# A four-stage sequence model: attention stacks moved in halves, a second pair of score banks for the last sequence, and its own instruction order for the first and last sequences

## The chip, the cores and the metric

One core of one Trainium2 chip runs the whole program. The metric is the device time of one execution in microseconds; the kernel before has a median of 1859.53 us over three runs (1855.02 to 1859.66). Of the engines, PE is TensorE, DVE VectorE, ACT ScalarE, POOL GpSimd, and SP issues the DMAs.

## What is computed

Sixteen sequences of 512 tokens with 128 channels pass through four residual stages, each behind a layernorm:

- **s**, a selective scan: `h = exp(delta*A)*h + x*x` over time for 256 channels with 16 states each, then the sum over states, gates, and a projection back to 128.
- **g**, eight linear experts with a softmax gate over the residual norms, of which the best two count.
- **t**, causal attention with 16 heads. Query and key of a head have 8 plain and 4 rotated dimensions; `attn = softmax(QK/sqrt(12)) V`, then a projection.
- **f**, a gated feed-forward net with three layers of width 512 and the output projection.

## The kernel before, in words

`one_pass` builds two phases. Phase one holds s, g and t of all sequences, phase two holds f. The engines are programmed by hand: each function such as `pe_scores` (L938) or `dve_scans` (L557) is a generator, a *strand*, that issues the instructions of one stage of one sequence on one engine, with its semaphore waits, in steps set off by `yield`. `in_order` (L197) merges the strands of an engine: step k of a strand of sequence b is due at `PERIOD * b + TIMES[name][k]`, and the step that is due first is issued next. The due times (L51 to L143) set nothing but this order. When a step runs is decided by its waits and by what stands ahead of it in the queue of its engine. Since a sequence's strands reach over some 3.5 periods, in the middle of phase one scans of one sequence, the experts of an earlier and the attention of a still earlier one are interleaved.

The parts around the change:

- *Scans.* Per sequence 32 scans (L566, DVE), whose decays come from ACT (L551) and whose results POOL adds up (L584). They need `dve_s_head` (L495), which needs the first projection `pe_s_head`.
- *Start.* `dve_setup` (L1124) step 0 makes the centering matrix (L1128) from the loaded identity; `pe_setup` (L1154) folds it into the weights of s, ACT copies the result back (L1096), and only then can the first projection run. Steps 3 and 4 (L1138), 5 (L1148) prepare the weights of g.
- *Experts.* `dve_g_gate` step 2 (L744 to L771) ends with the weights of the experts. PE transposes them (L647), ACT copies them (L701), PE adds the biases (L655), ACT copies (L706); then PE issues expert products (L669) into banks 3 and 4 in turn, and DVE accumulates each with four instructions (L790, `dve_g_experts`). Product e waits for the accumulation of product e-2.
- *Attention inputs.* `pe_t_proj` (L807) and `act_t_proj` (L850) make query and key of all heads in `parts`, DVE and POOL (L881, L901) the rotated rows in `rest`. Heads must lie on 12 neighbouring partitions, so `sp_rows` (L349) moves them by DMA into `stacks`, even heads at partition 0, odd heads at 64, eight pairs behind one another: two DMAs of 64 KB for the rotated queries (L360), two for the rotated key, broadcast over the pairs (L362), and four of 128 KB for the plain rows (L368). It first waits for the last score step of the sequence before, which reads the same buffer.
- *Scores.* `pe_scores` takes 4 groups of 4 heads in 5 steps each. A step fills a double bank of PSUM (`self.scores`, banks 5 and 6, 1024 columns); `act_scores` (L955) takes the exponential of it with one instruction (L967) into `probs`. There is one double bank, so each step waits for the exponential of the step before (`a_prob`).
- *Values.* Each group has three units (steps 0 and 1, 2 and 3, and 4). POOL masks the diagonal blocks of a unit (L1011), PE multiplies with the values (L1028). `probs` has two buffers: a unit's exponentials wait for the values of the unit two before. After a group ACT copies the sums (L982), PE transposes them (L1035), DVE divides (L1068, L1070). After the fourth group: PE, ACT and PE again (L1049, L986, L1055) and the addition to x (`dve_t_out`, L1078), then the moments for f (`dve_f_moments`, L380).

Phase two waits for all of phase one (`phase_one_over`). The program also holds a general version of both phases in a branch that the inputs here do not take.

The functions that the diff touches:

Of the kernel before, what the change touches and what calls it, by code (L numbers as in the profile page):

```python
# [6 lines left out]
F32 = mybir.dt.float32  # L7
# [7 lines left out]
P = 128  # L15
# [7 lines left out]
DQK = DH + DR  # L23
# [27 lines left out]
PERIOD, F_PERIOD = 78826, 24000  # L51
TIMES = {
    "sp_loads": [-193999],
    "sp_rows": [236612, 244449, 262646],
    "sp_weights": [202048],
    "pe_setup": [-253368],
    "pe_s_out": [105457],
    "pe_scores": [203061, 206712, 210127, 211906, 212752, 218421, 220191, 221756, 225635, 230028, 233012, 236030,
        238938, 243841, 244836, 246508, 250105, 253149, 258508, 260547],
    "pe_bound": [265919],  # L60
    "dve_setup": [-65717, -48779, -18943, -17968, -16808, -12885],
    "dve_scans": [-5373, -4435, -1891, 334, 3476, 5244, 7204, 9355, 13725, 15210, 17850, 18956, 19850, 22896, 23940,
        25115, 29162, 29883, 31506, 34450, 37022, 37715, 39471, 43460, 46148, 47755, 48770, 50392, 51830, 53721,
        55818, 56579],
    "dve_s_out": [36751, 66351, 104857],
    "dve_f_moments": [285358],
    "dve_bound": [265666],
    "act_setup": [-109930, -101590],
    "act_decays": [-9159, -8011, -5609, -4706, -4216, -2340, -1414, -1286, 2396, 2947, 3280, 4612, 4837, 7344, 10757,
        11123, 26812, 27582, 27750, 29700, 31063, 33980, 34333, 34908, 36535, 38255, 39294, 39719, 40895, 41965,  # L70
        43611, 44575],
    "act_inputs": [-9090, 28279],
    "act_f_rstd": [294212],
    "pool_setup": [-159627],
    "pool_sums": [-5156, -2015, 3236, 4530, 7688, 11440, 13004, 16496, 18832, 24903, 25813, 29142, 29865, 31310,
        34155, 34495, 35661, 37442, 38619, 41328, 41420, 41788, 43639, 46579, 47169, 48256, 51750, 53260, 54332,
        56586, 59092, 62805],
    "pool_t_proj": [181583],
    "pool_masks": [205555, 210959, 214428, 221911, 231307, 234364, 239298, 241162, 247591, 257454, 259145, 261183],
# [5 lines left out]
    "dve_clips": [205554, 210958, 214427, 221910, 231306, 234363, 239297, 241161, 247590, 257453, 259144, 261182],  # L85
    "pe_s_turn": [-44316],
    "pe_s_head": [-29204, -17779, -6800, 16442],
# [3 lines left out]
    "pool_s_head": [-19406, -10949, 18784, 22665],  # L91
    "pe_values": [210177, 216686, 219526, 221752, 223371, 231041, 234330, 237530, 242565, 246311, 247251, 251115,
        258893, 263255, 264524, 267412],
    "pe_t_out": [270351, 271838],
    "dve_values": [222049, 239132, 250423, 268172],
    "dve_t_out": [284589],
    "act_scores": [202759, 207082, 211090, 212302, 214034, 217813, 222387, 223555, 227340, 230817, 234204, 238260,
        240384, 242483, 245583, 249636, 251803, 255073, 257206, 258841],
    "act_nums": [220127, 235782, 250419, 265886, 272466],
# [17 lines left out]
    "pe_g_turn": [111532],  # L117
    "pe_g_residuals": [114116, 119481, 119533, 119540, 122328, 126496, 128548, 129135],
    "pe_g_own": [143450, 146011],
    "pe_g_experts": [149181, 150687, 152499, 155319, 156674, 157680, 161416, 164909],  # L120
    "act_g_rstd": [109296],
    "act_g_turned": [113955],
    "act_g_squares": [115694, 118311, 119742, 121869, 123757, 126271, 129317, 132198],
    "act_g_gate": [134222, 138635, 145715, 147184],
    "act_s_rstd": [-106834],
    "act_s_turned": [-35041],
    "act_s_xn": [-104074],
    "act_g_xn": [109881],
    "act_t_xn": [172512],
    "dve_g_norm": [106445],  # L130
    "dve_g_sums": [117932, 121419, 122771, 126327, 127060, 128048, 131606, 133569],
    "dve_g_gate": [134799, 136597, 141564],
    "dve_g_experts": [152123, 154366, 154898, 157601, 159574, 160538, 161592, 161722, 164119],
    "pe_t_turn": [173660],
    "pe_t_proj": [176180, 179691, 183932, 186365, 186842, 189324],
    "act_t_rstd": [171027],
    "act_t_turned": [174285],
    "act_t_proj": [184944, 186825, 187429],
    "dve_t_norm": [164962],
    "dve_t_proj": [176579, 178912, 188307, 191093],  # L140
    "pe_g_setup": [-14755, -8586, -4947, -2930, 3681, 17023],
    "act_g_setup": [-8024, -702, 28025, 63003, 104601],
    "pe_t_setup": [-3990, 26455, 88672],  # L143
    "act_t_setup": [30456, 43692, 102220],
# [1614 lines left out]
```

## Time and profile before

| | |
|---|---|
| median of three runs | 1859.53 us |
| the profiled execution | 1853.92 us |
| its span, first to last instruction | 1849.2 us |
| around the span | 4.7 us |
| mean granted clock of PE | 0.951 of full speed |
| busy over the span: PE, DVE, ACT, POOL | 82%, 83%, 70%, 60% |
| phase one, until the last addition to x | 0 to about 1454 us |
| first and last scan | at 29.8 and 1260.1 us |

Times in rows are us from the start of the span. A timeline row has start, duration, engine, line and operation, output<-inputs, sizes and a count; neighbours of one kind are merged, and in brackets stands how long the engine sat idle before and what released it.

### The profile page before, as it was taken

The numbers are of one execution on the slowest core, as the hardware profiler recorded it, in microseconds if no ns is written. First come the engines' busy times: TensorE is split into PE (matmuls) and PEld (weight loads), VectorE is DVE, ScalarE is ACT, GpSimd is POOL, SyncE is SP. The second block draws the span as 40 slices with busy tenths as digits, with TensorE's granted clock in tenths as the row PEclk, the third lists the DMA queues.
The fourth block names the chain that finished last, engine by engine and source line by source line (L and its number), as shares of the span: only waits on it lengthen the run. The fifth ranks groups of instructions, "written<-read, shape, count | busy, mean of one in ns | idle before, by whom it ended". The sixth has DMA issues, their size and how long they took to land. (4 is left out here: it accounts for less than half of the span.)

```text
span 1849.2 us, 24467 instructions
## 1 busy us (share of the span) xinstructions
PE 1518.6 (82%) x8039; PEld 807.2 (44%) x8039; DVE 1541.3 (83%) x2837; ACT 1286.7 (70%) x2176; POOL 1112.0 (60%) x987
## 2 busy tenths in 40 slices
PE   4246888888888888888888888888886699999997
PEld 2022333333433333343333334333332478888886
DVE  5899999999999999999999998996330488988883
ACT  5666898888888888888888888884543444444441
POOL 4885775858677585866758686674111255555552
PEclk9566999999999999999999999999998799999998
DMA  4000110101001010100101010010400000000000
GB/s 131 0 1 4 15 17 1 18 1 18 7 12 18 1 18 1 18 8 11 18 1 18 1 18 11 8 18 1 82 7 11 0 1 12 12 12 13 17 12 19
DMA packets 13773, 27.39 MB, mean 15 GB/s; under 512 B 3069, under 2 KB 3782, under 8 KB 13130
## 3 DMA queue, kind: packets, MB, share of 16 engines
q1 hardware_dynamic: 13642, 25.78, 7.2%
q8 instruction: 65, 1.06, 0.2%
q14 instruction: 66, 0.54, 0.1%
HBM read 9.00 MB, written 4.19 MB: 7 GB/s over the span
## 5 line engine op out<-in xcount | busy, mean ns | idle before, releaser
L584 POOL TENSOR_TENSOR sum_fast<-sum_fast,state_fast 128x512 f32<-128x512 f32 x448 | 574.0, 1281 | 122.1 <-DVE state_fast L566 84.1
L566 DVE TENSOR_TENSOR_SCAN state_fast<-state_fast,bank 128x512 f32<-128x512 f32 x512 | 602.1, 1201 | 1.6 <-ACT bank L535 1.6
L967 ACT ACTIVATE prob_fast<-bank 128x1024 f32<-128x1024 f32 x320 | 326.4, 1020 | 173.7 <-PE bank L951 172.1
L951 PE MATMUL bank<-stacks_fast 64*128 64x512 f32 (+3 forms) x2048 | 367.1, 467 | 71.3 <-ACT prob_fast L967 58.3
L551 ACT ACTIVATE state_fast<-chan_all_kept,neg_a_fast 128x512 f32<-128x512 f32 x512 | 342.8, 713 | 13.6 <-POOL sum_fast L584 12.4
L1011 POOL TENSOR_SCALAR_AFFINE_SELECT prob_fast<-prob_fast 128x512 f32<-128x512 f32 x256 | 166.4, 662 | 294.7 <-ACT prob_fast L967 293.8
L951 PEld LDWEIGHTS bank<-stacks_fast 64*128 64x128 f32 x2048 | 172.1, 187 | 282.0 <-ACT prob_fast L967 157.1
L1028 PE MATMUL bank<-prob_fast,v_ext_fast 128*32 128x512 f32 (+3 forms) x2048 | 175.9, 444 | 14.5 <-POOL prob_fast L1011 14.2
L638 PE MATMUL bank<-resid_m_fast,xnt_g_fast 128*128 128x512 f32 x256 | 145.2, 656 | 45.8 <-DVE gate_fast L719 32.0
L669 PE MATMUL bank<-we_t_fast,xnt_g_fast 128*128 128x512 f32 x256 | 141.3, 645 | 2.6 <-DVE own_fast L790 2.6
L1390 PE MATMUL bank<-cell_a_fast,w_all_fast 128*128 128x512 f32 x512 | 131.2, 398 | 0.3 <-POOL cell_a_fast L1586 0.3
L1414 PE MATMUL bank<-cell_b_fast,w_all_fast 128*128 128x512 f32 x512 | 129.9, 397 | 0.0
L1504 ACT ACTIVATE full_fast<-bank,sh_kept 128x512 f32<-128x512 f32 x64 | 44.1, 689 | 122.5 <-PE bank L1414 122.5
L790 DVE SCALAR_TENSOR_TENSOR x_res_kept<-bank,gate_fast,x_res_kept 128x128 f32<-128x128 f32 x256 | 86.8, 339 | 44.5 <-PE bank L669 44.5
L1586 POOL TENSOR_TENSOR cell_a_fast<-th_fast,cell_a_fast 128x512 fp32r<-128x512 f32 x64 | 104.9, 1639 | 29.7 <-ACT cell_a_fast L1468 29.7
L1390 PEld LDWEIGHTS bank<-cell_a_fast,w_all_fast 128*128 128x128 f32 x512 | 97.1, 190 | 24.3 <-issue 0.7
L1602 POOL TENSOR_TENSOR cell_c_fast<-full_fast,cell_c_fast 128x512 fp32r<-128x512 f32 x32 | 43.0, 1343 | 106.6 <-DVE cell_c_fast L1562 106.6
L1414 PEld LDWEIGHTS bank<-cell_b_fast,w_all_fast 128*128 128x128 f32 x512 | 95.0, 188 | 21.9
L1028 PEld LDWEIGHTS bank<-prob_fast,v_ext_fast 128*32 128x32 f32 x2048 | 48.5, 109 | 127.6 <-issue 76.4
L684 ACT ACTIVATE bank<-bank 128x512 f32<-128x512 f32 x128 | 74.7, 583 | 32.5 <-PE bank L638 30.7
L638 PEld LDWEIGHTS bank<-resid_m_fast,xnt_g_fast 128*128 128x128 f32 x256 | 41.5, 197 | 125.4 <-DVE gate_fast L719 96.6
L719 DVE TENSOR_REDUCE gate_fast<-bank 128x4 f32<-128x512 f32 x128 | 84.8, 663 | 11.9 <-ACT bank L684 11.9
(204 smaller groups left out, 2618.6 us busy)
## 6 DMA issues: line engine op xcount, KB each, us to landing
stacks_fast<-parts_fast SPq DMA_DIRECT2D x64, 128.0 KB
stacks_fast<-rest_fast SPq DMA_DIRECT2D x64, 64.0 KB
out_x<-f_out_fast SPq DMA_DIRECT2D x16, 256.0 KB, 2.0
x_res_kept<-in_x SPq DMA_DIRECT2D x1, 2048.0 KB, 14.7
chan_all_kept<-in_h_t SPq DMA_DIRECT2D x2, 1024.0 KB, 15.8
x_res_kept<-in_x SPq DMA_DIRECT2D x1, 1024.0 KB, 10.4
chan_all_kept<-in_w_t SPq DMA_DIRECT2D x3, 256.0 KB, 12.7
x_res_kept<-in_x SPq DMA_DIRECT2D x2, 256.0 KB, 2.9
```

The lines of the kernel that those rows point to most:

```text
L551: act.activation(self.state(b, i)[:], self.chan(b, ct)[1], ACT.Exp, scale=self.neg_a[:, i:i + 1]).then_inc(self.a_decay.sem)
L566: dve.tensor_tensor_scan(h[:], h[:], self.banks[0][:], 0.0, ALU.mult, ALU.add).then_inc(self.v_scan.sem)
L584: pool.tensor_tensor(total[:], total[:], h[:], ALU.add).then_inc(self.p_sum.sem)
L638: pe.matmul(banks[3 + half][:], xnt[:, k * P:(k + 1) * P], self.resid_m[:, half * 512:(half + 1) * 512], start=True, stop=True).then_inc(s ...
L669: pe.matmul(banks[3 + e % 2][:], xnt[:, k * P:(k + 1) * P], self.we_t[:, half * 512:(half + 1) * 512], start=True, stop=True).then_inc(sel ...
L951: ins = pe.matmul(self.scores[:, c:c + SEQ - P * kt], rows[:, 1, h // 2, P * kt:P * kt + P], rows[:, 0, h // 2, P * kt:SEQ], start=True, s ...
L967: act.activation(self.probs[u % 2][:, i * 1024:(i + 1) * 1024], self.scores[:], ACT.Exp, scale=SCALE).then_inc(self.a_prob.sem)
L1011: pool.affine_select(out=blocks, in_=blocks, compare_op=ALU.is_ge, fill=0.0, base=0, pattern=[[0, GROUP], [1, P]], channel_multiplier=-1). ...
L1028: ins = pe.matmul(bank[32 * j:32 * j + 32, P * kt:SEQ], v_ext[:, kt, h * VW:h * VW + 32], self.probs[u % 2][:, c:c + SEQ - P * kt], start= ...
L1390: ins = pe.matmul(banks[2 + mt % 2][:], w["h1_t"][:, c:c + P], self.f_a[s][k][:, i], start=(k + i == 0), stop=(k == MT - 1 and i == parts ...
L1414: ins = pe.matmul(banks[4 + mt % 2][:], w["h2_t"][:, c:c + P], self.f_h1[s][k][:, i], start=(k + i == 0), stop=(k == MT - 1 and i == parts ...
L1586: pool.tensor_tensor(cell[:, 1], th[:], cell[:, 0].bitcast(F32), ALU.subtract).then_inc(self.p_f_lo.sem)
```

## The change

1. *Halves.* `sp_rows` moves pairs 0 to 3 (the first eight heads) and then pairs 4 to 7, with its own semaphores `stack_lo` and `stack_hi`. A half is eight DMAs, each half as large as before. The low half waits only for score step 9 of the sequence before; score step 0 waits for the low half only, step 10 for the high one. The host lays out weight columns to match (`by_pair`).
2. *Double banks.* For sequence 15 alone, score steps alternate between two double banks, banks 3 and 4 (whose last user is the expert stage) and banks 5 and 6; a step waits for the exponential two steps before.
3. *Order.* All due times of phase one are new, and `EDGES` adds a shift per strand for sequences 0, 13, 14 and 15.

```diff
-PERIOD, F_PERIOD = 78826, 24000
+PERIOD, F_PERIOD = 78858, 24000
...
-    "dve_setup": [-65717, -48779, -18943, -17968, -16808, -12885],
+    "dve_setup": [-94988, -46358, -20989, -17676, -16326, -14489],
...
-    "dve_f_moments": [285358],
+    "dve_f_moments": [300701],
...
-    "dve_s_norm": [-169173],
-    "dve_s_head": [-20017, -12889, -7920, 12843, 17928, 21459],
+    "dve_s_norm": [-171059],
+    "dve_s_head": [-19777, -15497, -9844, 10929, 16708, 22079],
...
-    "act_s_head": [-28054, -16640, -13696, -11315, 5390, 16508, 20604, 22313],
+    "act_s_head": [-22126, -18333, -15652, -10894, 6618, 17515, 20463, 21378],
...
-    "dve_values": [222049, 239132, 250423, 268172],
-    "dve_t_out": [284589],
+    "dve_values": [219209, 237883, 250402, 268592],
+    "dve_t_out": [295932],
...
-    "pe_g_experts": [149181, 150687, 152499, 155319, 156674, 157680, 161416, 164909],
+    "pe_g_experts": [148444, 150157, 151620, 155582, 156829, 157978, 161983, 164085],
...
-    "dve_g_experts": [152123, 154366, 154898, 157601, 159574, 160538, 161592, 161722, 164119],
+    "dve_g_experts": [148823, 152617, 153586, 157048, 157334, 158263, 161453, 163412, 163789],
...
+EDGES = {
...
+    "dve_s_head": [-1343, 0, 231, 775], "dve_s_norm": [47049, -721, 714, -1415], "dve_s_out": [3873, 0, 180, 714],
...
+    "pe_scores": [0, 0, 0, -1501], "pe_t_out": [338, -711, 0, -79], "pe_t_proj": [-1734, 0, 0, 0],
+    "pe_t_turn": [-6589, 2763, 3868, 1299], "pe_values": [0, 0, 0, 1790], "pool_masks": [-23, 0, -493, -585],
...
+EDGE_OF = {0: 0, NSEQ - 3: 1, NSEQ - 2: 2, NSEQ - 1: 3}
+def place(period, name, b, k, edges):
+    shift = EDGES[name][EDGE_OF[b]] if edges and name in EDGES and b in EDGE_OF else 0
+    return period * b + TIMES[name][k] + shift
...
+        for half, moved in enumerate((self.stack_lo, self.stack_hi)):
+            cols = slice(half * PAIRS // 2, (half + 1) * PAIRS // 2)
+            yield
+            sp.wait_ge(self.p_t_rot.sem, self.p_t_rot.at(b))
+            if b:
+                sp.wait_ge(self.t_score.sem, self.t_score.at(b - 1, 5 * GROUPS // 2 * (half + 1) - 1))
+            else:
+                sp.wait_ge(self.p_stacks.sem, self.p_stacks.at())
             for r in (0, 64):
-                sp.dma_start(stacks[r:r + DH, i], parts[r:r + 64, i]).then_inc((self.stack_q, self.stack_k)[i].sem, 16)
+                n = r // 2 + half * NQ // 4
+                sp.dma_start(stacks[r + DH:r + DQK, 0, cols], rot[n:n + NQ // 4]).then_inc(moved.sem, 16)
+                sp.dma_start(stacks[r + DH:r + DQK, 1, cols], rot[NQ:ROPE_ROWS].unsqueeze(1).to_broadcast(
+                    [DR, PAIRS // 2, SEQ])).then_inc(moved.sem, 16)
+            for i in range(2):
+                yield
+                sp.wait_ge(self.a_t_qk.sem, self.a_t_qk.at(b, i))
+                for r in (0, 64):
+                    n = r + half * 32
+                    sp.dma_start(stacks[r:r + DH, i, cols], parts[n:n + 32, i]).then_inc(moved.sem, 16)
...
-                moved = (self.stack_q, self.stack_k)[i]
-                act.wait_ge(moved.sem, moved.at(b - 1, 1))
+                act.wait_ge(self.stack_lo.sem, self.stack_lo.at(b - 1, 7))
+                act.wait_ge(self.stack_hi.sem, self.stack_hi.at(b - 1, 7))
...
+        return self.doubles[0 if b == NSEQ - 1 and step % 2 else 1]
...
+                if n == 0 and g % 2 == 0:
+                    moved = self.stack_hi if g else self.stack_lo
+                    pe.wait_ge(moved.sem, moved.at(b, 7))
+                step = 5 * g + n
+                if b == NSEQ - 1 and step == 1:
+                    pe.wait_ge(self.v_g_acc.sem, self.v_g_acc.at(b, 31))
+                elif b == NSEQ - 1 and step > 1:
+                    pe.wait_ge(self.a_prob.sem, self.a_prob.at(b, step - 2))
+                elif b + step:
+                    pe.wait_ge(self.a_prob.sem, self.a_prob.at(b, step - 1))
```

The order that follows from the tables, for the steps that the prediction needs ("|" stands for scans, Ek for DVE's accumulation of expert product k, E8 for the sum after them, V for `dve_values`):

```
DVE, middle, before: E0 || E1 E2 | E3 | E4 V E5 | E6 E7 | E8 | moments_t
DVE, middle, after:  E0 E1 || E2 | E3 E4 | E5 V | E6 | E7 E8 || moments_t
DVE, before: sums3 | t_out sums4 | f_moments sums5 || sums6 ... gate2 V norm_s
DVE, after:  sums3 | sums4 | sums5 || sums6 ... t_out gate2 V f_moments norm_s
PE, sequence 15, before: s0 s1 s2 v0 s3 s4 v1 s5 v2 s6 v3 s7 v4 s8 s9 v5
PE, sequence 15, after:  s0 s1 s2 s3 s4 v0 s5 v1 s6 v2 s7 v3 s8 v4 s9 s10 v5
DVE, first steps, before: norm_s(0) norm_s(1) setup0 setup1 head0
DVE, first steps, after:  norm_s(0) setup0 norm_s(1) setup1 head0
```

## Rows read from the trace of the kernel before

**Rows 1.** Busy time by engine (PE, PEld, DVE, ACT, POOL), PEclk, DMA share, GB/s; a middle period, then the last scores.

```profile
541.50:622.00 80.50, 68.04 (x385) 29.71 (x385) 76.18 (x149) 69.11 (x119) 56.98 (x54) 1.00 0.08 11
1397.50:1447.00 49.50, 37.88 (x268) 15.83 (x268) 1.64 (x6) 22.33 (x25) 9.96 (x16) 0.90 0.00 1
```

**Rows 2.** Waits of DVE in 300:1100 us: total us, times, longest us.

```profile
DVE x_res_kept L790 <- PE bank L669: 18.0, 29, 1.4
DVE rden_fast L1068 <- PE bank L1035: 8.8, 10, 0.9
DVE chan_all_kept L514 <- ACT chan_all_kept L488: 4.7, 10, 0.5
DVE rest_fast L881 <- PE bank L816: 4.5, 10, 0.4
```

**Rows 3.** Timeline of DVE in one middle period.

```profile
525.56 0.84 DVE L380 BATCH_NORM_STATS2 bn_f_fast<-x_res_kept 128x6 f32<-128x128 f32 x4
...
548.60 0.35 DVE L790 SCALAR_TENSOR_TENSOR x_res_kept<-bank,gate_fast,x_res_kept 128x128 f32<-128x128 f32 x1 [1.04 <-PE bank L669]
...
559.62 0.26 DVE L1068 RECIPROCAL rden_fast<-bank 128x16 f32<-128x16 f32 x1 [0.88 <-PE bank L1035]
```

**Rows 4.** Timeline of PE, same stretch; 521.60 and 602.15 are score step 0 of two sequences.

```profile
521.60 1.13 PE L951 MATMUL bank<-stacks_fast 64*128 64x512 f32 x4
...
547.33 1.98 PE L669 MATMUL bank<-we_t_fast,xnt_g_fast 128*128 128x512 f32 x4
...
562.63 1.12 PE L669 MATMUL bank<-we_t_fast,xnt_g_fast 128*128 128x512 f32 x2
...
602.15 1.13 PE L951 MATMUL bank<-stacks_fast 64*128 64x512 f32 x4
```

**Rows 5.** DVE at the beginning of the span, with the ACT step that the same loads release.

```profile
6.27 0.23 ACT L1093 ACTIVATE neg_a_fast<-a_log_fast 128x32 f32<-128x32 f32 x1 [4.19 <-DMA w_out_fast<-in_w_out]
...
9.41 0.19 DVE L1128 TENSOR_SCALAR center_fast<-ident_kept 128x128 f32<-128x128 f32 x1
...
29.81 9.01 DVE L566 TENSOR_TENSOR_SCAN state_fast<-state_fast,bank 128x512 f32<-128x512 f32 x8 [0.35 <-ACT bank L535]
```

**Rows 6.** Timeline at the first score step of sequence 14, the last but one.

```profile
1319.48 1.98 PE L638 MATMUL bank<-resid_m_fast,xnt_g_fast 128*128 128x512 f32 x4 [0.54 <-DVE gate_fast L719]
...
1324.76 1.52 PE L951 MATMUL bank<-stacks_fast 64*128 64x512 f32 x4 [3.30 <-issue]
```

**Rows 7.** Timeline between the attentions of sequences 14 and 15.

```profile
1379.97 0.69 SPq L360 DMA_DIRECT2D stacks_fast<-rest_fast  x1
...
1383.70 3.99 SPq L368 DMA_DIRECT2D stacks_fast<-parts_fast  x4
...
1389.60 1.53 PE L1055 MATMUL bank<-w_o_fast,num_fast 128*128 128x128 f32 x8 [0.69 <-ACT num_fast L986]
...
1397.52 2.08 PE L951 MATMUL bank<-stacks_fast 64*128 64x512 f32 x4 [6.38 <-DMA stacks_fast<-parts_fast]
```

**Rows 8.** Timeline within the scores of sequence 15.

```profile
1412.12 1.13 PE L951 MATMUL bank<-stacks_fast 64*128 64x512 f32 x4
...
1415.43 0.66 PE L1035 MATMUL bank<-ident_kept,num_fast 128*128 128x128 f32 x4
...
1416.62 1.14 PE L951 MATMUL bank<-stacks_fast 64*128 64x384 f32 x8 [0.54 <-ACT prob_fast L967]
...
1417.81 1.02 ACT L967 ACTIVATE prob_fast<-bank 128x1024 f32<-128x1024 f32 x1 [1.24 <-PE bank L951]
...
1422.43 1.07 PE L1028 MATMUL bank<-prob_fast,v_ext_fast 128*32 128x384 f32 x16 [0.16 <-POOL prob_fast L1011]
...
1423.44 1.13 PE L951 MATMUL bank<-stacks_fast 64*128 64x512 f32 x4
...
1446.74 0.64 PE L1028 MATMUL bank<-prob_fast,v_ext_fast 128*32 128x256 f32 x8 [0.60 <-POOL prob_fast L1011]
```

**Rows 9.** The one line L740: duration ns min/median/max, first and last start us.

```profile
L740 DVE TENSOR_TENSOR gate_fast<-gate_fast x16: 191/1203/1209, 135.1 to 1336.5; 128x32 f32<-128x32 f32 x16
```

More of the change, by code:

```diff
@@ new lines @@
+    "act_g_rstd": [108225],
+    "act_g_turned": [112967],
+    "act_g_squares": [115764, 117057, 118967, 122562, 123481, 127459, 130176, 130535],
+    "act_g_gate": [134461, 138285, 145817, 146856],
+    "act_s_rstd": [-106092],
+    "act_s_turned": [-37648],
+    "act_s_xn": [-105174],
+    "act_g_xn": [109278],
+    "act_t_xn": [172336],
+    "dve_g_norm": [106960],
+    "dve_g_sums": [117369, 119221, 122317, 125256, 126753, 128740, 131699, 134197],
+    "dve_g_gate": [136286, 137675, 138806],
@@ L194, with in_order @@
 DONE = object()
-def in_order(period, strands):
-    parts = [[period * b + TIMES[name][0], rank, 0] for rank, (name, b, _) in enumerate(strands)]
+EDGE_OF = {0: 0, NSEQ - 3: 1, NSEQ - 2: 2, NSEQ - 1: 3}
+def place(period, name, b, k, edges):
+    shift = EDGES[name][EDGE_OF[b]] if edges and name in EDGES and b in EDGE_OF else 0
+    return period * b + TIMES[name][k] + shift
+def in_order(period, strands, edges=False):
+    parts = [[place(period, name, b, 0, edges), rank, 0] for rank, (name, b, _) in enumerate(strands)]
     for _, _, strand in strands:
@@ L209, in in_order @@
         else:
-            part[0], part[2] = period * b + TIMES[name][k + 1], k + 1
+            part[0], part[2] = place(period, name, b, k + 1, edges), k + 1
 class Program:
@@ L223, in __init__ @@
         self.signals |= {f"store{i}": Signal(sem(f"store{i}"), 1, NSEQ // STORES, 16) for i in range(STORES)}
-        self.banks = [ctx.enter_context(nc.psum_tensor(f"bank{i}", [P, 512], F32)) for i in range(5)]
-        self.scores = ctx.enter_context(nc.psum_tensor("bank5_6", [P, 1024], F32))
-        self.banks += [self.scores[:, 0:512], self.scores[:, 512:1024], ctx.enter_context(nc.psum_tensor("bank7", [P, 512], F32))]
+        self.banks = [ctx.enter_context(nc.psum_tensor(f"bank{i}", [P, 512], F32)) for i in range(3)]
+        self.doubles = [ctx.enter_context(nc.psum_tensor(n, [P, 1024], F32)) for n in ("bank3_4", "bank5_6")]
+        self.banks += [d[:, i * 512:(i + 1) * 512] for d in self.doubles for i in range(2)] + [ctx.enter_context(nc.psum_tensor("bank7", [P, 512], F32))]
         sb = self.room(ctx, "kept")
@@ L966, in act_scores @@
                         act.wait_ge(self.t_pv.sem, self.t_pv.at(bb, uu))
-                act.activation(self.probs[u % 2][:, i * 1024:(i + 1) * 1024], self.scores[:], ACT.Exp,
+                act.activation(self.probs[u % 2][:, i * 1024:(i + 1) * 1024], self.scores(b, 5 * g + n)[:], ACT.Exp,
                                scale=SCALE).then_inc(self.a_prob.sem)
@@ L1216, in sync_program @@
             strands.append(("sp_rows", b, self.sp_rows(b)))
-        in_order(PERIOD, strands)
+        in_order(PERIOD, strands, not general)
     def tensor_program(self, general):
@@ L1227, in tensor_program @@
             strands.append(("pe_bound", NSEQ - 1, self.pe_bound()))
-        in_order(PERIOD, strands)
+        in_order(PERIOD, strands, not general)
     def vector_program(self, general):
```

163 lines of the change are left out of this document (75 added, 88 removed).

## The prediction

> **What bounds the kernel now.** I read the busy time by engine over equal stretches first. In the middle of phase one two successive sequences stand 80.55 us apart (score step 0 at 521.60 and 602.15 [rows 4]), and of such a period DVE is busy 76.18 us, PE 68.0, ACT 69.1, POOL 57.0 [rows 1]. So the middle is DVE's, and what is left there is its idle time, 4.4 us per period. The view of DVE's waits names it: 18.0 + 8.8 + 4.7 + 4.5 = 36.0 us in 800 us [rows 2], that is 9.93 periods, so 3.6 us each. Half of that is DVE waiting for expert products, a quarter for the transposed attention sums. The timelines show where they fall: 1.04 us before the first accumulation of a sequence and 0.88 us before a `dve_values` [rows 3]; between the first and last expert product PE runs without a gap (547.33 to 562.63 [rows 4]).
>
> Both ends are different. At the beginning nothing overlaps: the first scan starts at 29.81 [rows 5], at the end of one chain. After the last scan at 1260.1 DVE is nearly idle (1.64 us of the last 49.5 [rows 1]), and the end is a chain through the last two sequences. It has three visible stalls. PE stands 3.30 us before score step 0 of sequence 14, whose only unmet wait is for the stacks [rows 6]. Before step 0 of sequence 15 it stands 6.38 us on those DMAs [rows 7]. And every score step of sequence 15 alternates with its exponential on the one double bank: a group of five steps takes 1423.44 - 1412.12 = 11.32 us, 2.26 per step, of which the product is 1.14 and the exponential 1.02 [rows 8].
>
> Differences under 0.3% (5.6 us) are no change below.
>
> **Part 1, start of the order.** DVE's center step at 9.41 needs only the first loads, which had landed by 6.27 [rows 5]; it stood behind the second sequence's moments, which wait for ACT. Moved ahead of them, it and the chain behind it (fold, copy, first projection, taps) start 9.41 - 6.27 = 3.14 us sooner. The moments still come before their user. I take **-3.1**. Bounds: 0, if something else holds the first scan, and perhaps 2 more, since the clipping now precedes the second half of the weights of g.
>
> **Part 2, the middle, 14 periods** (from about 120 us to the last scan). The order is nearly the same; four moves matter.
> - `f_moments` now stands between the gate and the first accumulation. That is 0.84 us for its statistics alone [rows 3], put where DVE idles 1.04: gain 0.84.
> - V stands one accumulation later, four instructions of 0.35, against a wait of 0.88 [rows 3]: gain 0.88.
> - `t_out` and `f_moments` leave the stretch of the sums, so DVE comes to the gate and the next taps sooner than ACT, and ACT's tap step itself moved behind an exponential. The old trace shows no wait there. The nearest row is DVE waiting for ACT's chain, 4.7 us in 9.93 periods [rows 2], 0.47. I charge 0.47. From below it can be 0; from above 3.3, one score step of 2.26 plus an exponential of 1.02 [rows 8].
> - E7 now stands before a values product on PE and behind one more scan on DVE: this relaxes the last wait for an expert. Counted at nothing.
>
> Net -0.84 - 0.88 + 0.47 = -1.25, times 14: **-17.5**. The most it can give is all waits, 3.6 x 14 = -51. With new waits of 3.3 and no gain it is +46, which I hold for unlikely, because 4.4 us per period stand idle on DVE, 12 on PE and 11 on ACT.
>
> Reordering also changes which short DVE operations meet a POOL operation: L740 takes 191 ns at best and 1203 at the median [rows 9]. One such meeting more or less per period is 1.0 x 14 = +-14 us. I have no sign for it; it goes into the range.
>
> **Part 3, halves, middle.** SP issues 16 DMAs per sequence instead of 8, at 0.69 us each for the present small ones [rows 7]: at most 5.5 us more SP time in 80, and nothing else stands in its queue there. The weight loads of phase two stay behind the stacks of sequence 14 and are needed only in phase two, at about 1454. Score step 10 now waits for the high half, two groups, so some 18 us or more, after step 0. ACT's copies and DVE's rotated product wait for both halves of the sequence before, a period old. All this costs nothing; without cover the DMAs would cost the 5.5 us.
>
> **Part 4, halves, end.** For sequence 15 the eight DMAs go from 1379.97 until step 0 can run at 1397.52 [rows 7], 17.5 us for all bytes. Half the bytes take half of it, landing about 1388.8; the plain keys, issued from 1383.70, are the last. Then the next limit is PE itself: the output product before it ends at 1389.60 + 1.53 = 1391.13. Gain 1397.52 - 1391.13 = **-6.4**. For sequence 14 the limit becomes the residual product, ending 1319.48 + 1.98 = 1321.46, against 1324.76 [rows 6]: **-3.3**. The expert stage of sequence 15 is interleaved behind it, so this moves the end. From below each is 0 (a half lands no sooner).
>
> The row says the transfers move with their bytes. "DMA: Bandwidth & Descriptors" of the Trainium skill, section Bandwidth, speaks against it: transfers under 64 KB are dominated by their descriptors, and the halves are of 32 and 64 KB. No run here has yet shown their landing. By that rule the low half would arrive with the present eight DMAs, and 9.7 us of the sum would go.
>
> **Part 5, double banks.** With two, step n waits for exponential n-2, so the alternation ends. The next limit is PE: per group five score steps of 1.14, three values units of 1.07, 1.07 and 0.64, and the transposes of 0.66 [rows 8], in sum 9.14 us. ACT needs 5 x 1.02 and a copy. POOL's masks lie beside PE, and the new order puts each values product behind one more score step to cover them. 11.32 - 9.14 = 2.2, over four groups **-8.7**. From above 0 gain, if the two `probs` buffers set the pace; from below -11, when the starts of PE overlap ends as now. The bank's former user, the expert stage of sequence 15, is long done. The granted clock averages 0.90 in this stretch [rows 1], of levels 1 and 0.5, so a fifth of it, 9.9 us, runs at 1.2 GHz; PE-bound steps feel this more, up to 4 us. It stays in the range.
>
> **Sum.** -3.1 - 17.5 - 3.3 - 6.4 - 8.7 = -39.0. Against the profiled execution's 1853.92 (span 1849.2 and 4.7 around it) that is 1814.9. That execution lies 5.6 under the median 1859.53, so a median may lie a little above; I say **1817**.
>
> **Rivals.**
> - *The middle stays as it is.* New waits take the place of old ones, as happens when an order is shifted between engines that are 84% busy or more. For it: the net is a third of the idle time only. Against it: the two largest waits get cover. 1814.9 + 17.5 = 1832, with the slack of the median 1835.
> - *The double banks don't pay.* Exponentials wait for values two units back, values for POOL's mask, the mask for the exponential: 1.02, a mask, 1.07 [rows 8] and a score step in between. If this closes at over 11 us per group, 8.7 is lost: 1824; together with the first rival 1841.
> - *The halves land no sooner* (the rule above, as a mechanism: time per DMA, not per byte). 1815 + 9.7 = 1825.
> - *Slower.* ACT's tap behind exponential 3 holds DVE's taps: 3.3 us per period at the upper bound, and the gains of 1.72 not realised. 1853.9 - 21.5 + 46 = 1878. It decides when the middle loses over 21.5 / 14 = 1.5 us per period. For it: ACT has only 11 us free per period and takes long runs in order. Against it: DVE is the fuller engine, and its order is the one that was relaxed.
> - *No change.* A middle that loses 1.1 to 1.9 us per period, or an early change of alignment that eats the ends' gain.
>
> **Chances.** All parts as summed 0.42 (own range 1800 to 1828); middle unchanged 0.27 (1828 to 1843); double banks void 0.07; halves void 0.09; no change 0.07; slower 0.08. So faster 0.85, same 0.07, slower 0.08. The range 1798 to 1845 leaves out the last two and a little of the sum's lower end.
>
> **What would show it.** Center step at about 6.3 us and first scan near 26.7. Period under 80.55, with the 1.04 and 0.88 gone from DVE's waits and something small new before L504. Step 0 of sequence 15 directly behind L1055, no DMA wait; its groups at about 9 us. I am wrong if the period is 80.5 or more, if step 0 still waits for a stack, or if an exponential of sequence 15 is mostly held by L1028.

## The result, and the profile after

The kernel after takes **1785.45 us** at the median of four runs (1783.74 to 1786.55), the kernel before 1859.28 beside it: ratio 0.961, interval 0.959 to 0.9624. The profiled executions are 1786.55 and 1853.92, their spans 1781.5 and 1849.2. The prediction said 1817, 1798 to 1845: the direction was right, the time is 12.5 us below the range. One of the four executions of run e8 below took 2901.47 us, over 1100 us more than the others, and is left out of its time.

The lines of code have moved: the scan is L598, scores L992, exponentials L1008, values L1069, masks L1052, expert products L701 and their accumulation L822, the gate L772 to L803, the addition of the attention output L1119.

Where the span went, from the same rows in both traces (before in [rows 5] to [rows 8], the last scans at 1260.1 and 1221.3):

| stretch | before | after | difference | forecast |
|---|---|---|---|---|
| start to first scan | 29.8 | 27.0 | -2.8 | -3.1 |
| first to last scan | 1230.3 | 1194.3 | -36.0 | -17.5 |
| last scan to step 0 of sequence 14 | 64.6 | 60.2 | -4.5 | -3.3 |
| to step 0 of sequence 15 | 72.8 | 62.0 | -10.7 | -6.4 |
| to its last values product | 49.2 | 34.6 | -14.6 | -8.7 |
| to the end | 402.5 | 403.4 | +0.9 | 0 |

Windows of the kernel after, columns as in [rows 1]: a middle period, and the scores of sequence 15.

```profile
552.72:630.51 77.79, 67.66 (x388) 29.94 (x385) 74.63 (x150) 68.97 (x119) 56.47 (x54) 1.00 0.05 11
...
1343.50:1378.12 34.62, 32.34 (x261) 14.74 (x261) 3.40 (x15) 21.80 (x25) 9.96 (x16) 1.00 0.02 5
```

The period, the distance between the score steps 0 of two sequences, went from 80.55 to 77.79. DVE's idle time in it fell from 4.4 to 3.2 us, but its *busy* time fell too, from 76.18 to 74.63, with the same instructions. That part was not in the sum. During the scores of sequence 15 PE is now busy 32.3 of 34.6 us, and the granted clock is 1.00.

DVE's waits after, 300 to 1100 us, columns as in [rows 2]:

```profile
DVE x_res_kept L822 <- PE bank L701: 12.8, 33, 1.2
DVE rest_fast L914 <- PE bank L848: 5.3, 10, 0.5
DVE v_ext_fast L922 <- PE bank L860: 3.6, 10, 0.4
DVE chan_all_kept L536 <- ACT chan_all_kept L500: 2.3, 9, 0.3
DVE chan_all_kept L546 <- ACT chan_all_kept L520: 0.4, 1, 0.4
```

They sum to 24.4 us over 10.28 periods, 2.4 each, against 3.6. The other half of the period's gain is in short operations of the gate and in the skip product. The groups of DVE by line, same stretch (count, busy us, mean ns, idle before), first the kernel before:

```profile
L602 DVE SCALAR_TENSOR_TENSOR y_all_fast<-chan_all_kept,skip_d_fast 128x512 f32<-128x512 f32 x20 | 28.8, 1442 | 0.0
L740 DVE TENSOR_TENSOR gate_fast<-gate_fast 128x32 f32<-128x32 f32 x10 | 12.1, 1205 | 0.3
L771 DVE TENSOR_TENSOR gate_fast<-gate_fast 128x32 f32<-128x32 f32 x10 | 10.1, 1015 | 0.3
L767 DVE SCALAR_TENSOR_TENSOR gate_fast<-kept_all_kept 128x4 f32<-128x4 f32 x10 | 9.6, 962 | 0.3
...
L761 DVE SCALAR_TENSOR_TENSOR gate_fast<-gate_fast 128x32 f32<-128x32 f32 x9 | 1.7, 192 | 0.3
```

And after, where they are L634, L772, L803, L799 and L793:

```profile
L634 DVE SCALAR_TENSOR_TENSOR y_all_fast<-chan_all_kept,skip_d_fast 128x512 f32<-128x512 f32 x20 | 17.6, 882 | 0.0
...
L803 DVE TENSOR_TENSOR gate_fast<-gate_fast 128x32 f32<-128x32 f32 x10 | 10.2, 1024 | 0.3
L793 DVE SCALAR_TENSOR_TENSOR gate_fast<-gate_fast 128x32 f32<-128x32 f32 x10 | 8.5, 846 | 0.3
...
L799 DVE SCALAR_TENSOR_TENSOR gate_fast<-kept_all_kept 128x4 f32<-128x4 f32 x10 | 4.7, 466 | 0.3
...
L772 DVE TENSOR_TENSOR gate_fast<-gate_fast 128x32 f32<-128x32 f32 x10 | 2.3, 234 | 0.3
```

Per period: two skip products -1.1, L740 -1.0, L767 -0.5, L761 +0.65. What stretches them shows in the timeline of the kernel after, DVE and POOL:

```profile
525.15 1.27 POOL L554 TENSOR_TENSOR chan_all_kept<-chan_all_kept 128x512 f32<-128x512 f32 x1 [2.35 <-ACT chan_all_kept L508]
...
525.62 0.85 DVE L793 SCALAR_TENSOR_TENSOR gate_fast<-gate_fast 128x32 f32<-128x32 f32 x1
...
527.14 1.27 POOL L622 TENSOR_TENSOR chan_all_kept<-sum_fast,chan_all_kept 128x512 f32<-128x512 f32 x1
...
527.43 1.03 DVE L803 TENSOR_TENSOR gate_fast<-gate_fast 128x32 f32<-128x32 f32 x1
```

L793 ends at 526.47 and L554 at 526.42; L803 ends at 528.46 and L622 at 528.41. Alone such an operation takes 0.19 us; one that begins while POOL works ends with POOL's, to 0.05 us. I call this a meeting. The longer L540 and L634 (128x512) meet POOL too and end 0.3 and 0.55 us behind it.

The tail of the kernel after, PE:

```profile
1280.43 1.12 PE L670 MATMUL bank<-resid_m_fast,xnt_g_fast 128*128 128x512 f32 x2 [0.54 <-DVE gate_fast L751]
1281.49 1.13 PE L992 MATMUL bank<-stacks_fast 64*128 64x512 f32 x4
...
1342.41 1.16 PE L1096 MATMUL bank<-w_o_fast,num_fast 128*128 128x128 f32 x8 [0.69 <-ACT num_fast L1027]
1343.50 1.99 PE L992 MATMUL bank<-stacks_fast 64*128 64x512 f32 x8
...
1352.14 1.13 PE L992 MATMUL bank<-stacks_fast 64*128 64x512 f32 x4
...
1360.45 1.13 PE L992 MATMUL bank<-stacks_fast 64*128 64x512 f32 x4
```

Both steps 0 (1281.49, 1343.50) follow the product ahead of them without a wait, and a group takes 1360.45 - 1352.14 = 8.31 us.

### The profile page after: what moved, and what is told of

It reads as the page before. It is cut to its first block and busy times, and to the rows that moved or that the text cites. A ratio compares the mean times of both kernels' runs of the same rounds, so it can differ in the third digit from the quotient of the medians.

```text
span 1781.5 us, 24641 instructions
## 1 busy us (share of the span) xinstructions
PE 1502.4 (84%) x8039; PEld 807.3 (45%) x8039; DVE 1519.0 (85%) x2837; ACT 1284.4 (72%) x2176; POOL 1103.6 (62%) x987
## 2 busy tenths in 40 slices
DMA packets 14543, 27.41 MB, mean 15 GB/s; under 512 B 3837, under 2 KB 4550, under 8 KB 13898
## 3 DMA queue, kind: packets, MB, share of 16 engines
q8 instruction: 65, 1.06, 0.3%
## 5 line engine op out<-in xcount | busy, mean ns | idle before, releaser
L598 DVE TENSOR_TENSOR_SCAN state_fast<-state_fast,bank 128x512 f32<-128x512 f32 x512 | 602.7, 1202 | 0.7 <-ACT bank L567 0.7
L1008 ACT ACTIVATE prob_fast<-bank 128x1024 f32<-128x1024 f32 x320 | 326.0, 1020 | 122.1 <-PE bank L992 111.7
L992 PE MATMUL bank<-stacks_fast 64*128 64x512 f32 (+3 forms) x2048 | 361.4, 462 | 50.0 <-ACT prob_fast L1008 46.6
L1052 POOL TENSOR_SCALAR_AFFINE_SELECT prob_fast<-prob_fast 128x512 f32<-128x512 f32 x256 | 159.9, 636 | 293.6 <-ACT prob_fast L1008 292.1
L992 PEld LDWEIGHTS bank<-stacks_fast 64*128 64x128 f32 x2048 | 170.7, 185 | 250.0 <-ACT prob_fast L1008 150.8
L1069 PE MATMUL bank<-prob_fast,v_ext_fast 128*32 128x512 f32 (+3 forms) x2048 | 177.7, 442 | 8.1 <-POOL prob_fast L1052 7.5
L670 PE MATMUL bank<-resid_m_fast,xnt_g_fast 128*128 128x512 f32 x256 | 137.2, 637 | 34.5 <-DVE gate_fast L751 33.1
L701 PE MATMUL bank<-we_t_fast,xnt_g_fast 128*128 128x512 f32 x256 | 133.7, 633 | 2.5 <-DVE own_fast L822 2.5
L822 DVE SCALAR_TENSOR_TENSOR x_res_kept<-bank,gate_fast,x_res_kept 128x128 f32<-128x128 f32 x256 | 87.4, 341 | 38.4 <-PE bank L701 38.4
L1069 PEld LDWEIGHTS bank<-prob_fast,v_ext_fast 128*32 128x32 f32 x2048 | 47.1, 108 | 138.8 <-issue 83.9
L1431 PEld LDWEIGHTS bank<-cell_a_fast,w_all_fast 128*128 128x128 f32 x512 | 97.2, 190 | 24.4 <-issue 0.7
L751 DVE TENSOR_REDUCE gate_fast<-bank 128x4 f32<-128x512 f32 x128 | 84.9, 664 | 9.1 <-ACT bank L716 9.1
L670 PEld LDWEIGHTS bank<-resid_m_fast,xnt_g_fast 128*128 128x128 f32 x256 | 42.7, 193 | 106.1 <-DVE gate_fast L751 77.1
```

Of the source, the lines that this page charges most:

```text
L598: dve.tensor_tensor_scan(h[:], h[:], self.banks[0][:], 0.0, ALU.mult, ALU.add).then_inc(self.v_scan.sem)
L670: pe.matmul(banks[3 + half][:], xnt[:, k * P:(k + 1) * P], self.resid_m[:, half * 512:(half + 1) * 512], start=True, stop=True).then_inc(s ...
L701: pe.matmul(banks[3 + e % 2][:], xnt[:, k * P:(k + 1) * P], self.we_t[:, half * 512:(half + 1) * 512], start=True, stop=True).then_inc(sel ...
L992: ins = pe.matmul(self.scores(b, step)[:, c:c + SEQ - P * kt], rows[:, 1, h // 2, P * kt:P * kt + P], rows[:, 0, h // 2, P * kt:SEQ], star ...
L1008: act.activation(self.probs[u % 2][:, i * 1024:(i + 1) * 1024], self.scores(b, 5 * g + n)[:], ACT.Exp, scale=SCALE).then_inc(self.a_prob.sem)
L1052: pool.affine_select(out=blocks, in_=blocks, compare_op=ALU.is_ge, fill=0.0, base=0, pattern=[[0, GROUP], [1, P]], channel_multiplier=-1). ...
```

## The experiments

Theory A: the order made the middle, in equal parts by covered waits and by fewer meetings of DVE with POOL; at the end the stall for the stacks and the one bank were worth more than their visible gaps. Rivals: the halves helped the middle; the durations are DVE's own; the end came from the order alone.

**The order alone (e1).** The kernel before with the new common due times: all lists of TIMES as in the change but `sp_rows`, and no EDGES.

```diff
-PERIOD, F_PERIOD = 78826, 24000
+PERIOD, F_PERIOD = 78858, 24000
...
-    "dve_bound": [265666],
+    "dve_bound": [268700],
```

> The kernel before with the new period and the new common due times of every strand (only the three due times of the DMA rows stay, and DVE's bound step is put behind the last values); no shifts for the edges, whole stacks, one double bank. Theory A, the middle is the work of the order alone: the distance of score steps 0 in the middle falls from 80.55 to 77.8 us, 14 x 2.75 = 38 us less, so about 1821 us, give or take 6 for the ends, whose order is only the common one. Theory B, the halves have a part in it (no SP queue or DMA burst behind the scores): the distance stays above 79 and the time above 1835.

1817.17 us, ratio 0.978 (0.9761 to 0.98). First to last scan it takes 1193.0 us, even a little less than the kernel after; its periods are 77.8 to 78.2. So the gain of the middle is the order's. The halves have at most a small part: the periods here change between 77.8 and 78.2, where the kernel after has 77.8 throughout, and over the twelve periods from score step 0 of sequence 0 this comes to 4.4 us (936.4 against 932.0).

**One strand of the order (e2).** `f_moments` to behind the gate.

```diff
-    "dve_f_moments": [285358],
+    "dve_f_moments": [300701],
-    "act_f_rstd": [294212],
+    "act_f_rstd": [319896],
```

> The kernel before with one strand moved: the moments for f from among the sums to behind the gate (and the ACT step that reads them, to its new place). Theory A, the wait alone: the 1.04 us before the first accumulation are covered by 0.84, the period falls by 0.8 to about 79.7, 1848 us. Theory B, meetings with POOL decide: the sum of the DVE durations changes by a different amount than the wait, because the operations behind the new place start at other times against POOL; L602 (mean 1.40 us, 0.74 at least) falls towards 0.9, twice per period, and the period falls by 1.5 or more, or the busy time grows and eats the 0.84.

1855.49 us, ratio 0.9978 (0.9966 to 0.999). A period of full clock is 80.0; six of the first thirteen are 81.4 to 81.7, each with a short fall of the granted clock (see the last section). The wait before the first accumulation was *not* covered: it is 1.16 us in the period at 380 us. The accumulation began 6.0 us after the end of the gate where it had begun 5.1 us after it. PE's timeline in that period shows why:

```profile
379.62 0.61 PE L647 MATMUL bank<-ident_kept,gate_fast 128*9 128x128 f32 x4 [0.79 <-DVE gate_fast L771]
...
381.15 1.06 PE L1028 MATMUL bank<-prob_fast,v_ext_fast 128*32 128x512 f32 x8 [0.92 <-DVE attn_fast L1070]
382.14 1.15 PE L655 MATMUL bank<-bias_e_fast,w9t_fast 9*128 9x128 f32 x8
```

Between the transposes of the gate (L647) and the biases (L655) PE has a values product, L1028, and it now waits 0.92 us for DVE's division (L1070, part of `dve_values`). In the kernel before it does not wait. The moments stand ahead of this `dve_values` here; in the full change they stand behind it. So e2 put the strand at a place that the change does not use, and the 0.92 us put the product, and with it the accumulation, back by what the moments would have covered. The gain came from durations: around the gate L740, L771 and L602 shrank by 0.7, 0.6 and 2 x 0.3, and L508 by 0.3, while L751 grew by 1.0 and L761 by 0.5. This was the term for which I had claimed a mechanism, and this run does not bear it out. (In the full change the wait is 0.58.)

**The center step alone (e3).**

```diff
-    "dve_setup": [-65717, -48779, -18943, -17968, -16808, -12885],
+    "dve_setup": [-95000, -48779, -18943, -17968, -16808, -12885],
```

> The kernel before with the center step alone moved ahead of the moments of the second sequence. Theory A: center step at about 6.3 us, first scan at 26.7 to 27.0 in place of 29.8, and the whole 2.8 to 3.1 us reach the end: 1856.5. Theory B: DVE is not free early in the first sequence, or another input holds the first scan: the time stays within 1 us.

Center step at 6.34, first scan at 28.04, 1.8 earlier and not 3.1. The center step (L1128) began 3.1 us sooner but takes 1.50 us where it took 0.19:

```profile
0.83 6.92 POOL L1199 MEMSET stacks_fast<- 128x8192 f32 x1
...
6.34 1.50 DVE L1128 TENSOR_SCALAR center_fast<-ident_kept 128x128 f32<-128x128 f32 x1 [1.45 <-DMA w_out_fast<-in_w_out]
```

It ends at 7.84, 0.09 us behind POOL's fill of `stacks`: a meeting with POOL again, and the lost 1.3 us. In the kernel after the step begins at 6.82 and also ends at 7.84.

1858.12 us against 1858.54, ratio 1.0 (0.9985 to 1.0016): in the time an effect of 1.8 us can't be told from none. In the trace the gain is carried on: score step 0 of sequence 4 is at 518.85, against 521.60 in the kernel before and 520.95 in e4, whose start is the same as before.

**Double banks in the old order (e4).**

```diff
+        return self.doubles[0 if b == NSEQ - 1 and step % 2 else 1]
...
-                if b + g + n:
-                    pe.wait_ge(self.a_prob.sem, self.a_prob.at(b, 5 * g + n - 1))
+                step = 5 * g + n
+                if b == NSEQ - 1 and step == 1:
+                    pe.wait_ge(self.v_g_acc.sem, self.v_g_acc.at(b, 31))
+                elif b == NSEQ - 1 and step > 1:
+                    pe.wait_ge(self.a_prob.sem, self.a_prob.at(b, step - 2))
+                elif b + step:
+                    pe.wait_ge(self.a_prob.sem, self.a_prob.at(b, step - 1))
```

> The kernel before with the second pair of score banks for the last sequence and nothing else: old order of its steps. Theory A, the one double bank was the limit: the group of five steps falls from 11.3 to 9.1 us, -8 us, 1851. Theory B, the banks need the new order: in the old one a values product stands directly behind the score step whose exponential it does not yet have with its mask, so PE stops there instead, and the group stays at 10.3 or more: -4 us or less.

1850.23 us, ratio 0.9959 (0.9946 to 0.9972), -8. Its PE timeline within sequence 15:

```profile
1411.50 1.07 PE L1037 MATMUL bank<-prob_fast,v_ext_fast 128*32 128x384 f32 x16 [1.55 <-POOL prob_fast L1020]
1412.50 1.13 PE L960 MATMUL bank<-stacks_fast 64*128 64x512 f32 x4
...
1422.72 1.13 PE L960 MATMUL bank<-stacks_fast 64*128 64x512 f32 x4
```

The group is 10.2 us. More than half of what the banks can give is lost to 1.55 us of waiting for POOL's mask: theory B's mechanism. The whole is still -8, since the steps ahead of the first sums (step 0 to the first division) gain 4 of it (14.7 us against 18.6).

**Meetings with POOL (e5).** The second channel step and the gate product are cut in the same way.

```diff
-            pool.tensor_tensor(xc, tmp, xc, ALU.mult).then_inc(self.p_s_xc.sem)
+            pool.tensor_tensor(xc[:, 0:1], tmp[:, 0:1], xc[:, 0:1], ALU.mult).then_inc(self.p_s_xc.sem)
...
-                pool.tensor_tensor(total[:], total[:], h[:], ALU.add).then_inc(self.p_sum.sem)
+                pool.tensor_tensor(total[:, 0:1], total[:, 0:1], h[:, 0:1], ALU.add).then_inc(self.p_sum.sem)
```

> The kernel before with POOL's running sums, gate products and the two channel steps cut to one of their 512 columns (the rest of these sums and products is left out; the first sum of each 16, the masks and the rotation stay whole). DVE's own instructions, and every wait between engines, stay. POOL is not the fuller engine (57 of 80.5 us), so its shorter instructions alone should not change the period. Theory A, short DVE operations are held while a POOL operation runs: L740 falls from 1.20 to 0.19 us, L602 from 1.40 to 0.74, L767 and L771 from 0.96 and 1.02 to 0.19, L508 to 0.43; together 2 x 0.66 + 1.0 + 0.77 + 0.83 + 2 x 0.37 = 4.7 us of DVE per period, so the period comes near 76 and the time near 1800. Theory B, the durations are those of the operations themselves: they stay as they are, and the period stays over 80.

One run, 1818.23 us, with the kernel before at 1856.72 beside it. DVE's groups by line, 300 to 1100 us:

```profile
L602 DVE SCALAR_TENSOR_TENSOR y_all_fast<-chan_all_kept,skip_d_fast 128x512 f32<-128x512 f32 x20 | 14.6, 729 | 0.0
L514 DVE TENSOR_TENSOR chan_all_kept<-bank,chan_all_kept 128x512 f32<-128x512 f32 x20 | 13.8, 692 | 24.5 <-ACT chan_all_kept L488 24.5
...
L740 DVE TENSOR_TENSOR gate_fast<-gate_fast 128x32 f32<-128x32 f32 x10 | 1.9, 192 | 0.3
L771 DVE TENSOR_TENSOR gate_fast<-gate_fast 128x32 f32<-128x32 f32 x10 | 1.9, 192 | 0.3
L767 DVE SCALAR_TENSOR_TENSOR gate_fast<-kept_all_kept 128x4 f32<-128x4 f32 x10 | 1.7, 168 | 0.3
```

DVE's code is that of before, and each held operation fell to its floor (L508 too, to 0.43 us): theory A, shown. The Trainium skill, "SBUF — State Buffer", section Who interferes with whom, has this rule: a DVE instruction with two inputs in SBUF and a GpSimd instruction that reads SBUF lock each other out, and the second waits. This trace agrees, and so does L822 of the kernel after, which reads one input from PSUM and stays between 0.32 and 0.35 us. Two inputs in SBUF are not the only case, though: L508 and the center step have one, and they are held as well. But the period went to 78.0 and not to 76: 2 us of the 4.7 went straight into a new wait of DVE for ACT (L514, 24.5 us).

**One bank in the new order (e6).** Every step of sequence 15 waits for the exponential of the step before.

```diff
-        return self.doubles[0 if b == NSEQ - 1 and step % 2 else 1]
+        return self.doubles[1]
...
-                elif b == NSEQ - 1 and step > 1:
-                    pe.wait_ge(self.a_prob.sem, self.a_prob.at(b, step - 2))
```

> The kernel after with one double bank for the last sequence too; order and halves stay. Theory A, the banks are worth what the groups show: five steps go from 8.3 back to 11.3 us, four groups, +12, about 1797. Theory B, as in the kernel before, where the banks alone gave 8: +8, about 1793, the rest of the 12 being the order, which stays.

1810.63 us, ratio 0.975 (0.972 to 0.9779): 25 us over the kernel after, at least twice what the theories said. PE and ACT within sequence 15:

```profile
1358.19 1.13 PE L988 MATMUL bank<-stacks_fast 64*128 64x512 f32 x4 [1.21 <-ACT prob_fast L1004]
...
1359.25 1.07 PE L1065 MATMUL bank<-prob_fast,v_ext_fast 128*32 128x384 f32 x16
1360.44 1.02 ACT L1004 ACTIVATE prob_fast<-bank 128x1024 f32<-128x1024 f32 x1 [2.31 <-PE bank L1065]
...
1371.72 1.13 PE L988 MATMUL bank<-stacks_fast 64*128 64x512 f32 x4 [1.21 <-ACT prob_fast L1004]
```

The exponential waits for the values product ahead of it (its half of `probs`), and the next score step for the exponential: score, values and exponential run one after the other. With e4 this makes the table of the group of five steps:

| | old order | new order |
|---|---|---|
| one bank | 11.32 | 13.53 |
| two banks | 10.22 | 8.31 |

Order and banks must be counted together. The new order costs 2.2 us per group without the banks and gives 1.9 with them.

**Whole stacks (e7)** in the kernel after: `sp_rows`, its waits, due times and layout as before.

```diff
-        for half, moved in enumerate((self.stack_lo, self.stack_hi)):
...
+        for r in (0, 64):
+            sp.dma_start(stacks[r + DH:r + DQK, 0], rot[r // 2:r // 2 + NQ // 2]).then_inc(self.stack_r.sem, 16)
...
-                if n == 0 and g % 2 == 0:
+                if n + g == 0:
```

> The kernel after with the stacks moved whole, by the eight DMAs and with the waits of before; order and double banks stay. Theory A: score step 0 of sequence 15 waits again for the plain keys, some 6 us behind L1096, and step 0 of sequence 14 some 3 us, +8 to +10, about 1794; nothing changes in the middle (period 77.8). Theory B, the order has already taken the wait (the inputs are projected earlier): under +3.

1804.58 us, ratio 0.9718 (0.9689 to 0.9748): 19 us over the kernel after, twice theory A. PE, and a window:

```profile
1281.59 1.12 PE L665 MATMUL bank<-resid_m_fast,xnt_g_fast 128*128 128x512 f32 x2 [0.54 <-DVE gate_fast L746]
1288.58 2.08 PE L987 MATMUL bank<-stacks_fast 64*128 64x512 f32 x4 [5.86 <-issue]
...
1359.91 4.33 PE L987 MATMUL bank<-stacks_fast 64*128 64x512 f32 x16 [5.66 <-issue]
```

```profile
1284.00:1294.00 10.00, 5.42 (x8) 1.71 (x8) 0.75 (x3) 1.60 (x2) 0.00 (x0) 0.51 0.87 242
```

Both stalls are back, as 5.9 and 5.7 us, and around each the granted clock is at 0.5 for 10 us: the same four matmuls take 2.08 us where they take 1.13. What set the clock back is not shown; the second time it fell at 1352.5, 1.8 us ahead of the stall. From the starts of the same products in both traces the two stalls are 11.5 us and the slower matmuls about 4.5. At sequence 14 the stall is longer than the 3.3 of before, since the new order brings PE there sooner (14.2 us after the first DMA issue, where it was 16.8). The last scan is at 1222.5, 1.2 later; the rest of the 16.7 us of span is the tail's.

**No shifts at the edges (e8).**

```diff
-        in_order(PERIOD, strands, not general)
+        in_order(PERIOD, strands)
-    "dve_bound": [246417],
+    "dve_bound": [268700],
```

> The kernel after with the common due times for all sequences, none of the shifts for sequences 0, 13, 14 and 15 (DVE's bound step is put behind the last values); halves and double banks stay. Theory A: the first scan comes 3 us later, the last sequences lose some 8 more through values products that stand directly behind their score steps and experts that come late, +11, about 1796. Theory B, the shifts of the end are worth nothing: +3 at most, about 1788.

1792.44 us at the median of three executions, ratio 0.9654 (0.9616 to 0.9691), 7 us over the kernel after and between the two theories. The first scan is at 30.7, but the last at 1220.7, no later than after. Until score step 0 of sequence 12 it is still 3.1 us behind (1133.27 against 1130.15); the next period is 77.8 here and 80.8 in the kernel after, where shifts begin and where its clock also falls once, at 1207. The group of sequence 15 takes 1374.62 - 1364.39 = 10.2 us with the 1.55 us of waiting for the mask, as in e4. So the shifts of sequence 15, of which `pe_scores` and `pe_values` put the scores ahead of the values, make 8.3 of 10.2.

The three prices don't add. Taken out one by one, banks, halves and shifts cost 25, 19 and 7 us, 51 in all; e1, which lacks all three, is only 31.7 us over the kernel after.

**Two edits from the meetings (e9, e10)**, each one due time in the kernel after, the last step of `pool_sums` and `dve_t_out`, and both together (e11).

```diff
-        58696, 64691],
+        58696, 60000],
```
```diff
-    "dve_t_out": [295932],
+    "dve_t_out": [296700],
```

> The kernel after with one due time of POOL changed: the gate product (L622) of a sequence stands ahead of the next sequence's first channel step (L554), not behind it. POOL stood idle 2.35 us before L554. Theory A, meetings of short DVE operations with POOL set the period: POOL runs L622 in that idle time, and L799 (0.47) or L803 (1.03) no longer meet it; the period falls from 77.8 by up to 0.8, 14 periods, 1774 to 1785. Theory B: L554 and L557 only move up and meet the same operations, or L622 now meets L634's input chain; the period stays within 0.2, 1785.

> The kernel after with one due time of DVE changed: the addition of the attention output (L1119) stands behind the end of the gate, not ahead of it. The gate's chain starts 0.6 us earlier against POOL's L554. Theory A, meetings decide: L793 (0.85) ends before L554 begins and falls to 0.19, L803 meets the end of a mask instead of L622 and falls from 1.03 to 0.5, L799 grows from 0.47 to 1.0; together -0.6 per period, -8, 1777. Theory B: the order of DVE's waits alone matters, and no wait changes: 1785.

> The kernel after with both edits of the two runs before. Theory A, meetings: the two are not additive, since both move the same operations against each other; between 0 and -1.3 per period, 1767 to 1785. Theory B: no change, 1785.

They give 1779.22, 1780.13 and 1785.37 us; ratios 0.9574 (0.9542 to 0.9606), 0.9572 (0.9535 to 0.9609), 0.9615 (0.9579 to 0.9651). The periods are 77.0, 77.1 and 77.5. In the first, the last product of the gate no longer meets anything:

```profile
L801 DVE TENSOR_TENSOR gate_fast<-gate_fast 128x32 f32<-128x32 f32 x10 | 1.9, 192 | 0.3
```

In the second, L793, L799 and L803 came out as forecast (0.19, 1.0, 0.5), and the period fell by 0.7 (forecast 0.6); the time fell by 5, not 8:

```profile
L799 DVE SCALAR_TENSOR_TENSOR gate_fast<-kept_all_kept 128x4 f32<-128x4 f32 x10 | 9.7, 966 | 0.3
L803 DVE TENSOR_TENSOR gate_fast<-gate_fast 128x32 f32<-128x32 f32 x10 | 5.4, 538 | 0.3
...
L793 DVE SCALAR_TENSOR_TENSOR gate_fast<-gate_fast 128x32 f32<-128x32 f32 x10 | 1.9, 192 | 0.3
```

With both, the product of the gate at L780 (0.19 in the kernel after) takes 0.84, and the gain is nearly gone; that meeting was not forecast. The first two lie 5 to 6 us under the kernel after. Their intervals against before overlap its own a little, so the profiles' periods carry this more than the times.

**Without the shifts of sequence 0 (e12).**

```diff
-EDGE_OF = {0: 0, NSEQ - 3: 1, NSEQ - 2: 2, NSEQ - 1: 3}
+EDGE_OF = {NSEQ - 3: 1, NSEQ - 2: 2, NSEQ - 1: 3}
```

> The kernel after without the shifts of sequence 0; the others stay. Theory A, DVE is the bound from the first scan on, so what the first scan loses (27.0 to 30.7 us) arrives whole at the end: +3.7, about 1789. Theory B: the middle takes up the slack of the first sequences, and the end moves by less than 1.

First scan at 28.43, last at 1221.1, 1786.38 us: 1 us or nothing. The expected 3.7 us at the first scan was wrong too; the center step is ahead in the common times as well.

## Why the prediction was wrong in size

The step that failed is the middle's: meetings of DVE with POOL were put at nothing in the sum, and they gave 1.5 us per period. A second step, the stalls and the scores at the end, had its mechanism right and its size too small, 18.4 us where 29.8 were measured.

- **Part 1, start:** the first scan moved by -2.8 (forecast -3.1), but the center step alone gave 1.8 of it, because it met POOL's fill (e3); the rest is the order of the weights' preparation behind it. The traces of e3 and e8 carry the difference well into the middle. That it reaches the end was assumed and isn't shown: the times of e3 and e12 say 0 to 1 us.
- **Part 2, middle, the step that failed.** The waits gave 1.26 per period, the sum said 1.25, and that agreement is luck: the first accumulation gave 0.5 and not 0.84, the wait at L514, 0.4 to 0.5, went away uncounted, and `v_ext` and the taps took 0.6 back. The meetings with POOL, "I have no sign for it; it goes into the range", gave 1.5 per period, 21 us, over the +-14 allowed. One meeting was allowed; five operations moved. e5 and e10 show that single meetings can be worked out beforehand: the trace gives for each short operation its start and the POOL operation that runs then. For two edits together (e11) that failed.
- **Part 3:** right; going back to whole stacks makes the last scan 1.2 us later (e7), a trifle.
- **Part 4:** mechanism right, size off. Step 0 of both sequences runs where I said, right behind L670 and L1096, but the halves are worth 19 us in e7 (16.7 of span) and not 9.7. The slower clock around each stall wasn't priced, about 4.5 us; in the kernel before it averages 0.54 from 1389.6 to 1408. And in the new order the stall of sequence 14 would have been 5.9, not 3.3: a term that I had priced in the old order. (The plain rows issued from 1383.70 are the queries, the keys follow at 1386.31; that changes nothing in the sum.)
- The rule of the Trainium skill ("DMA: Bandwidth & Descriptors", section Bandwidth) that transfers under 64 KB are dominated by their descriptors doesn't give what the prediction made of it. Only the rotated rows' DMAs, 32 KB, are under that size. And a half has half of the packets too: the profile's pages count 13773 packets in the kernel before and 14543 after, and 768 of the difference are under 512 B. So this rule gives no later landing of a half. Measured: with whole stacks step 0 runs 9.8 us after the last issue ends (1350.1 to 1359.9 in e7), with the low half at most 5.5 (1338.0 to 1343.5), and the number of DMAs is eight in both.
- **Part 5:** -14.6 in the stretch. PE's sum of 9.14 per group was the right limit but too high by 0.8: successive matmuls overlap their shown durations, starts are 1.06 apart where 1.13 is shown. That makes 3.0 per group, 12 in all. I put the rest, 2.6, down to the full clock (1.00 against 0.90), which no run isolates.
- Of the rivals, none held: the middle changed, the banks paid, the halves landed sooner, no new wait of note came.
- The profiled run of before lay 5.6 under its median; I took back 2 of these. Medians moved 73.8, the profiled pair 67.4, so 3.2 us of the miss (31.6 in the median, 28.4 in the profiled pair) lie in which execution was profiled.

## What to carry to other kernels

Where VectorE is the bound, list its short operations with a mean over their minimum, and look which GpSimd operation runs at each one's start: that is as much a term of the sum as a wait, and one due time was worth 6 us here, two together nothing. A stall for DMA at the end of the work can cost more than its length: two of them, 11.5 us, went with 4.5 us of slower matmuls. An order and the buffers that it needs must be priced together: for the scores of the last sequence the banks alone gave 1.1 us per group, the order alone lost 2.2, both gave 3.0.

## What was not expected of the hardware

- A DVE operation of 0.19 us takes up to 1.2 us beside POOL's, and ends with it (L740, L803). The moments (L412, 0.26 to 0.30 us) and the accumulation, which reads PSUM (L822), aren't stretched.
- The granted clock falls to 0.5 for 3 to 4 us at a time in the middle as well, and a period with such a fall is 1.6 us longer. In e4 the falls begin at 567.2, 891.5, 973.4 and 1055.4, each in a period of 82.0 to 82.2; ahead of the first PE had stood 1.12 us for an exponential and 0.69 for a mask. The windows of two successive periods of e4:

```profile
542.80:625.00 82.20, 69.70 (x386) 30.13 (x384) 76.33 (x150) 69.15 (x119) 57.07 (x55) 0.98 0.07 11
625.00:705.60 80.60, 68.10 (x386) 29.77 (x384) 76.28 (x150) 69.19 (x119) 57.11 (x55) 1.00 0.08 11
```

  Between 200 and 1200 us the traces with the old order (the kernel before, e2, e3, e4, e5) have 0, 6, 3, 4 and 3 such falls, and the nine traces with the new order have none. So the new order may also gain by this, beyond the waits and the meetings: the profile of the kernel before shows no fall there and lies 5.6 us under its median. This is a likely source of the spread of the kernel before (1852 to 1864 us). It rests on one trace of each kernel, and nothing was run to bring the falls about or to remove them.
